# Reading the experts' bounds between pieces of the first tiles, in a two-block transformer kernel with a routed feed-forward layer

## The reference

```python
x = x + tanh(g_xattn[0]) * L0_xattn(layernorm(x), ctx)
x = x + tanh(g_ffn[0])   * L0_ffn(layernorm(x))
x = x + tanh(g_xattn[1]) * L1_xattn(layernorm(x), ctx, ctx)
x = x + tanh(g_ffn[1])   * L1_ffn(layernorm(x))       # Fourier weights

# L0_ffn, H = 256, F = 1024, E = 8, two experts a row
probs = softmax(x @ gate_w.T);  topw, sel = top_k(probs, 2);  topw /= sum(topw)
gu = einsum('th,efh->etf', x, gate_up_w);  gate, up = gu[..., :F], gu[..., F:]
expert_out = einsum('etf,ehf->eth', up * gelu(gate), down_w)
out = sum over the two experts of weight * expert_out
```

## Time and profile before

| | |
|---|---|
| median of 3 runs | 1301.15 us (1299.22 to 1301.48) |
| profiled execution, its own time | 1300.25 us |
| its span, first to last instruction | 1298.7 us |
| mean granted TensorE clock | 0.947 |
| TensorE busy | 1189.8 us, 92% |
| VectorE busy | 892.5 us, 69% |
| ScalarE busy | 569.6 us, 44% |
| first tile's load issued | 382.83 us |
| first matmul of the expert stage | 397.63 us |
| last half-tile load | 939.7 us |

### The profile page before, as it was taken

One profiled execution on the slowest core, in us unless ns is written; L12 is line 12 of the kernel. 1 busy time (PEld: TensorE's weight loads), 2 busy tenths in 40 slices (PEclk: granted clock), 3 DMA queues, 4 the chain that ended last, 5 costly groups with the idle time before them and its releaser, 6 DMA issues.

```text
span 1298.7 us, 34926 instructions
## 1 busy us (share of the span) xinstructions
PE 1189.8 (92%) x11816; PEld 992.6 (76%) x11816; DVE 892.5 (69%) x2696; ACT 569.6 (44%) x1184; POOL 263.2 (20%) x394
## 2 busy tenths in 40 slices
PE   4898989898867999999999999999997999999996
PEld 3677777776646888888888888888885777777774
DVE  4687677777645667675766767686565787787872
ACT  4565555555513242242424233242223665666652
POOL 5023242333331000000000000000004344444310
PEclk9899788888878999999999999999999999999998
DMA  9443333333433213021121313101012232222210
GB/s 293 183 162 107 117 116 124 128 101 110 150 133 138 91 37 127 33 95 61 71 94 38 122 34 126 34 25 46 26 47 81 66 93 87 81 82 85 82 34 21
DMA packets 82745, 119.58 MB, mean 92 GB/s; under 512 B 27326, under 2 KB 52558, under 8 KB 80589
## 3 DMA queue, kind: packets, MB, share of 16 engines
q1 hardware_dynamic: 64172, 60.32, 14.8%
q0 software_dynamic: 12848, 49.05, 11.3%
q10 hardware_dynamic: 5616, 8.78, 1.8%
HBM read 63.81 MB, written 47.58 MB: 86 GB/s over the span
## 4 chain that ended last, share of the span: by engine, by line
PE 80%; DVE 7%; issue 6%; SPq 2%; ACT 2%; DMA 1%; another core or an unknown queue 0%; POOL 0%; DVEq 0%; POOLq 0%; ACTq 0%
PE bank L1773 28%; PE bank L1786 14%; PE bank L1600 7%; PE bank L1534 6%; PE bank L1456 5%; PE bank L1587 3%; PE bank L1517 3%; PE bank L1519 3%; PE bank L1476 3%; PE bank L1540 2%; PE bank L1611 1%; DVE bm L1094 1%; PE bank L1598 1%; PE bank L1560 1%; PE bank L1502 1%
## 5 line engine op out<-in xcount | busy, mean ns | idle before, releaser
L1773 PE MATMUL bank<-tiles,we 128*128 128x256 f16 (+1 forms) x3744 | 392.6, 258 | 11.1 <-issue 10.2
L1773 PEld LDWEIGHTS bank<-tiles,we 128*128 128x128 f16 x3744 | 324.7, 98 | 51.1 <-issue 18.6
L947 ACT ACTIVATE tiles<-bank 128x256 f32<-128x256 f32 (+1 forms) x312 | 109.3, 353 | 330.9 <-PE bank L1773 312.2
L1786 PE MATMUL bank<-we,tiles 128*128 128x256 f16 x1608 | 223.5, 273 | 5.5 <-DVE tiles L1386 4.4
L1382 DVE SCALAR_TENSOR_TENSOR tiles<-bank,tiles 128x256 f32<-128x256 f32 (+1 forms) x312 | 120.2, 385 | 143.6 <-ACT tiles L947 138.6
L1786 PEld LDWEIGHTS bank<-we,tiles 128*128 128x128 f16 x1608 | 148.7, 98 | 40.8 <-DVE tiles L1386 17.0
L1534 PE MATMUL bank<-qT,kbd 128*128 128x256 f16 x960 | 161.6, 288 | 1.9 <-issue 1.2
L1094 DVE TENSOR_REDUCE bm<-bank 128x4 bf16<-128x308 f32 x256 | 118.2, 475 | 62.9 <-PE bank L1519 48.8
L471 DVE TENSOR_TENSOR pr<-pr 128x512 f16<-128x512 f32 x160 | 108.4, 682 | 30.9 <-ACT pr L809 25.0
L1388 DVE TENSOR_TENSOR tiles<-tiles 128x256 f16<-128x256 f32 (+1 forms) x312 | 121.1, 388 | 11.2 <-DVE tiles L1386 0.7
L1534 PEld LDWEIGHTS bank<-qT,kbd 128*128 128x128 f16 x960 | 97.4, 104 | 21.5 <-issue 1.8
(11 more groups left out here) (196 smaller groups left out, 1678.2 us busy)
## 6 DMA issues: line engine op xcount, KB each, us to landing
expert_out<-zeros SPq DMA_DIRECT2D x16, 896.0 KB
wes<-in_guT POOLq DMA_DIRECT2D x9, 1024.0 KB, 5.1
tiles<-expert_in SPq DMA_DIRECT2D x29, 256.0 KB, 2.6
pr<-in_guT POOLq DMA_DIRECT2D x7, 1024.0 KB
yg<-in_dnT POOLq DMA_DIRECT2D x7, 1024.0 KB
expert_out<-tiles ACTq DMA_DIRECT2D x28, 256.0 KB, 2.3
expert_in<-zeros POOLq DMA_DIRECT2D x8, 640.0 KB, 13.0
xin<-in_x SPq DMA_DIRECT2D x16, 256.0 KB
```

What stands on the lines that cost most here:

```text
L947: act.activation(ge[:, fc % 2, 0:n * P], bank[1 + fc % 3][:, 0:n * P], ACT.Gelu, scale=INV).then_inc(s.gelu, 1)
L1773: last = pe.matmul(bank[1 + fc % 3][:, half * S:half * S + w * P], gate_up[:, par, c, i, col:col + P], xT[:, j, c, 0:w * P], start=n == 0, ...
L1786: last = pe.matmul(bank[4 + t][:, 0:D], act16[:, fc % 4, i, t * P:(t + 1) * P], we[:, par, 2, j, fc * D:(fc + 1) * D], start=fc == 0 and n ...
```

## The change

TensorE, ScalarE and VectorE no longer read their values in one go. Each gets a function `next_bound()` that reads the next value that it has not read yet, and calls it between pieces of expert 0's first two tiles. TensorE calls it after each `up` from the third on and after each `down` (14 in tile 0, the remaining two in tile 1). VectorE calls it once at the end of each piece of tiles 0 and 1. ScalarE calls it once after each piece in tile 0 and twice in tile 1. Expert 0's bound, zero, becomes a constant on ScalarE and VectorE. SyncE's three values for expert 0 are read before `pad_first` and the wait for the scatters instead of after it.

```diff
-            def tile_rows(e):
+            def tile_bounds(e):
                 t0 = sp.value_load(tbl[0:1, bass.ds(e, 1)], min_val=0, max_val=TILES)
                 t1 = sp.value_load(tbl[0:1, bass.ds(e + 1, 1)], min_val=1, max_val=TILES)
                 tw = sp.value_load(tbl[0:1, bass.ds(e + (2 * E + 1), 1)], min_val=1, max_val=TILES)
+                return t0, t1, tw
+
+            def tile_rows(e, bounds):
+                t0, t1, tw = bounds
...
             sp.wait_ge(s.tiles_counted, 1)
+            first = tile_bounds(0)
             pad_first(sp)
             for k in range(2):
                 sp.wait_ge(s_scat[k], 64 * (NB // 2))
             sp.wait_ge(s.first_padded, 16)
-            tile_rows(0)
+            tile_rows(0, first)
             sp.wait_ge(s.padding_zeroed, 16 * (E - 1))
             with sp.Fori(1, E) as e:
-                tile_rows(e)
+                tile_rows(e, tile_bounds(e))
...
                     if part == 0 and par is not None and fc < 6:
                         next_high(e, par, fc)
+                    if e == 0 and part < 2:
+                        for _ in range(part + 1):
+                            next_bound()
                 x_hi(g + 1)
...
-            bound = [act.value_load(tbl[0:1, e:e + 1], min_val=4 if e else 0, max_val=TILES)
-                     for e in range(E + 1)]
-            end = [act.value_load(tbl[0:1, 2 * E + 1 + e:2 * E + 2 + e], min_val=3, max_val=TILES - 1)
-                   for e in range(E)]
-            offset = [act.value_load(tbl[0:1, 3 * E + 1 + e:3 * E + 2 + e], min_val=0,
-                                     max_val=OUT_ROWS - SHORT * P) for e in range(E)]
+            bound, end, offset = [0], [], []
+
+            def next_bound():
+                if len(offset) < E:
+                    e = 3 * E + 1 + len(offset)
+                    offset.append(act.value_load(tbl[0:1, e:e + 1], min_val=0, max_val=OUT_ROWS - SHORT * P))
+                elif len(bound) <= E:
+                    e = len(bound)
+                    bound.append(act.value_load(tbl[0:1, e:e + 1], min_val=4, max_val=TILES))
+                elif len(end) < E:
+                    e = 2 * E + 1 + len(end)
+                    end.append(act.value_load(tbl[0:1, e:e + 1], min_val=3, max_val=TILES - 1))
...
                             next_low(e, par, k)
                         done += LOW_PIECES[part][fc]
+                    if e == 0 and part < 2:
+                        next_bound()
                 x_low(g + 1)
...
             dve.wait_ge(s.tiles_counted, 1)
-            bound = [dve.value_load(tbl[0:1, e:e + 1], min_val=4 if e else 0, max_val=TILES)
-                     for e in range(E + 1)]
-            end = [dve.value_load(tbl[0:1, 2 * E + 1 + e:2 * E + 2 + e], min_val=3, max_val=TILES - 1)
-                   for e in range(E)]
+            bound, end = [0], []
...
-            bound = [0] + [pe.value_load(tbl[0:1, e:e + 1], min_val=1, max_val=TILES)
-                           for e in range(1, E + 1)]
-            end = [pe.value_load(tbl[0:1, 2 * E + 1 + e:2 * E + 2 + e], min_val=1, max_val=TILES)
-                   for e in range(E)]
+            bound, end = [0], []
...
                     up(par, g, fc, w)
                     if fc == 2:
                         t_x(g + 1)
+                    next_bound()
                     down(par, g, fc - 2, w)
+                    next_bound()
                 down(par, g, FC - 2, w)
+                next_bound()
                 down(par, g, FC - 1, w)
+                next_bound()
```

More of the change, by code:

```diff
@@ L940, in next_high, with expert_tile @@
                                scale=SCALE).then_inc(s.next_high, 1)
-            def expert_tile(e, g, par, part, first, t0, tw, n=QT):
+            def expert_tile(e, g, par, part, t0, n=QT):
                 for fc in range(FC):
@@ L958, in expert_tile @@
                 if n == QT:
-                    row = out_row(first + (g * S - t0 * S), S)
+                    row = out_row(offset[e] + (g * S - t0 * S), S)
                     act.dma_start(rows(ys_d, row), ysb).then_inc(s.expert_rows_stored, 16)
                 else:
-                    row = out_row(first + (g * P + tw * P - t0 * S), P)
+                    row = out_row(offset[e] + (g * P + end[e] * P - t0 * S), P)
                     act.dma_start(ys_d[bass.ds(row, P), :], ysb[:, 0]).then_inc(s.expert_rows_stored, 16)
-            bound = [act.value_load(tbl[0:1, e:e + 1], min_val=4 if e else 0, max_val=TILES)
-                     for e in range(E + 1)]
@@ L967, in _ @@
-            end = [act.value_load(tbl[0:1, 2 * E + 1 + e:2 * E + 2 + e], min_val=3, max_val=TILES - 1)
-                   for e in range(E)]
-            offset = [act.value_load(tbl[0:1, 3 * E + 1 + e:3 * E + 2 + e], min_val=0,
-                                     max_val=OUT_ROWS - SHORT * P) for e in range(E)]
-            def expert(e, par):
[L973 to L979, removed]
+            bound, end, offset = [0], [], []
@@ L981, in _ @@
+            def expert(e, par):
+                t0 = bound[e]
+                expert_tile(e, t0, par, 0, t0)
+                expert_tile(e, t0 + 1, par, 1, t0)
+                with act.Fori(t0 + 2, end[e]) as g:
+                    expert_tile(e, g, par, 2, t0)
+                with act.Fori(end[e], bound[e + 1]) as g:
+                    expert_tile(e, g, par, 2, t0, 1)
             x_hi(0)
@@ L1393, in expert_tile, with next_bound @@
                         done += LOW_PIECES[part][fc]
+                    if e == 0 and part < 2:
+                        next_bound()
                 x_low(g + 1)
             def expert(e, par):
-                t0, t1, tw = bound[e], bound[e + 1], end[e]
+                t0 = bound[e]
                 expert_tile(e, t0, par, 0)
                 expert_tile(e, t0 + 1, par, 1)
-                with dve.Fori(t0 + 2, tw) as g:
+                with dve.Fori(t0 + 2, end[e]) as g:
                     expert_tile(e, g, par, 2)
-                with dve.Fori(tw, t1) as g:
+                with dve.Fori(end[e], bound[e + 1]) as g:
                     expert_tile(e, g, par, 2, 1)
             dve.wait_ge(s.tiles_counted, 1)
-            bound = [dve.value_load(tbl[0:1, e:e + 1], min_val=4 if e else 0, max_val=TILES)
-                     for e in range(E + 1)]
-            end = [dve.value_load(tbl[0:1, 2 * E + 1 + e:2 * E + 2 + e], min_val=3, max_val=TILES - 1)
-                   for e in range(E)]
+            bound, end = [0], []
+            def next_bound():
+                if len(bound) <= E:
+                    e = len(bound)
+                    bound.append(dve.value_load(tbl[0:1, e:e + 1], min_val=4, max_val=TILES))
+                elif len(end) < E:
+                    e = 2 * E + 1 + len(end)
+                    end.append(dve.value_load(tbl[0:1, e:e + 1], min_val=3, max_val=TILES - 1))
             x_low(0)
@@ L1789, in down, with next_bound @@
                 last.then_inc(s.down, 1)
-            bound = [0] + [pe.value_load(tbl[0:1, e:e + 1], min_val=1, max_val=TILES)
-                           for e in range(1, E + 1)]
-            end = [pe.value_load(tbl[0:1, 2 * E + 1 + e:2 * E + 2 + e], min_val=1, max_val=TILES)
-                   for e in range(E)]
+            bound, end = [0], []
+            def next_bound():
+                if len(bound) <= E:
+                    e = len(bound)
+                    bound.append(pe.value_load(tbl[0:1, e:e + 1], min_val=1, max_val=TILES))
+                elif len(end) < E:
+                    e = 2 * E + 1 + len(end)
+                    end.append(pe.value_load(tbl[0:1, e:e + 1], min_val=1, max_val=TILES))
             def tile(e, g, w):
```

## The result

The changed kernel takes 1288.58 us (median of 6 runs, 1285.64 to 1291.53) against 1300.54 for the kernel before (median of 6 on the same chip, 1299.22 to 1304.1): ratio 0.9908, 95% interval 0.9891 to 0.9924. That is 12.0 us, between 9.9 and 14.2. The profiled execution is the fastest of the six, 1285.64 us with a span of 1284.1; mean granted clock 0.953.

What follows compares the result with a forecast made beforehand. The prediction took the engines' `tbl` reads ahead of expert 0's first tile as the bound; 11.3 (start) + 1.45 (clock) - 0.85 (added) = 11.9 us gained, giving 1289.3 us, range 1286.8 to 1293.8 with rivals.

Steps and rivals of the forecast that it cites:

- What bounds it: Ahead of expert 0's first tile: TensorE's `tbl` loads hold `t_x(0)` and ScalarE's hold `x_hi(0)`; the wait is not for data.
- SyncE: Before the first tile's load: reads move ahead of the padding, which becomes the last wait; worth 0.5 us, not 1.7.
- The new start: First matmul of expert 0's first tile at about 386.3 instead of 397.63: gain 11.3 us.
- The clock: First 36 matmuls at full clock take 4.09 us instead of 5.79; less 0.25 lost, net gain 1.45 us.
- Rival 1: At the first tile the clock falls all the same, costing 1.7 to 3.4 us: 1291.0 to 1292.7; chance 0.2.
- the one at 984.8: Stretch of the profile before with TensorE busy 1.74 us and 1.66 idle, where the clock kept 1.00.
- What it adds: Reads between pieces of tiles 0 and 1 cost 0.35 + 0.4 + 0.1 = 0.85 us; bounds nothing and 10.5.
- Rival 2: In tile 0 each of eight loads behind a `down` costs 0.66, 5.3 us for 0.75 counted: 1293.8; chance 0.12.
- rival 3: Slower: each load among engine instructions waits until its engine has drained, 5.9 us above now: 1307; chance 0.03.
- What it triggers: Tile 1's load runs beside GpSimd's 1 MB fetch, landing at 388.5 or 391.4; taken as nothing, 0.9 kept for the range.
- The range: Forecast's own range for the kernel's time: 1287.3 (nothing added and 1 us between runs) to 1290.9 (late tile load and 0.7).

Runs made afterwards that it cites:

- SyncE's part alone: Kernel before with only SyncE's three reads of expert 0 moved ahead of the padding, the other engines reading in one go; ratio 1.0004.
- TensorE's with SyncE's: Changed kernel, but ScalarE's 24 and VectorE's 16 reads stand in one go ahead of the first tile; ratio 0.9998.
- the three engines' together: Changed kernel with SyncE's reads put back where they were in the kernel before; ratio 0.9924.
- The run with the padding first: Changed kernel with the padding's DMA issued ahead of SyncE's three reads, which still precede the wait for the scatters; ratio 0.9903.
- The sixteen reads in a row: Changed kernel with TensorE's 16 reads all behind up(4) of tile 0 instead of one behind each piece; ratio 0.9989.

## Why the prediction was right

The time on record, 1289.3, lies 0.7 above the measured median; the forecast gain was 11.9 and the measured one 12.0, with an interval of over 2 us on either side. The traces give 10.6, and one term of the sum was wrong by more than the number is off: by the prediction's own price for a falling clock, 1.7 at least, the time would have been 1291.0 or more. So the closeness to 0.7 us is luck; that the start is what the reads hold, and that reads between pieces cost next to nothing, is not. By the steps:

- *What bounds it.* Right. SyncE's part alone and TensorE's with SyncE's give nothing (ratios 1.0004 and 0.9998), and the three engines' together give nearly all.
- *SyncE.* Right: the load at 5.25 for a forecast of 5.2 (382.3 less 377.1), and the padding as the new last wait. The run with the padding first shows what that order costs: 1.3 us at the first matmul, and 3.0 at tile 1 (25.32 against 28.29), since the clock held there.
- *The new start.* 11.3 forecast, 11.05 and 10.9 in the two pairs of traces. The transposes came 0.2 late: the load landed after 2.65 and not 2.56, and 0.14 went by behind it.
- *The clock.* This step failed: 1.45 forecast, -0.3 and -0.1 in the two pairs (the block from the first matmul to the second transposes took 5.63 and 5.62 before, 5.92 and 5.71 after). Rival 1, given 0.2, is what happened in both profiles of the changed kernel and in that without SyncE's part. The price I gave it, 1.7 at least, is about what the comparison with the held clock shows: 5.92 and 5.71 against 4.25, so 1.7 and 1.5. The reason given for the chance, that the new stretch would be like the one at 984.8, did not hold.
- *What it adds.* 0.85 forecast, 0.35 measured: tile 0 from its second transposes 12.46 to 12.89, tile 1 from 16.54 to 16.46. The end of tile 0 cost the 0.4 that I counted. The 0.35 after `down(0)` did not come, with the clock fallen or, in the runs with the padding first, held: I had shifted the activation with the matmuls that it followed, but the ACT_TABLE_LOAD no longer waits for them. It runs at 385.13, straight behind `x_hi`, and not after the first piece of `up`, which brings the first Gelu forward by up to its 1.28 us. It isn't where the reads stand that does this: with ScalarE's reads in one go ahead of `x_hi` it also runs straight behind it (397.18 + 0.60, 397.79). What these kernels share, and the kernel before and SyncE's part alone lack, is expert 0's bound as a constant; I had costed that edit at nothing. The traces show where the wait stands: before the change ScalarE's queue waits for the first piece of `up` in an operation of its own (L946, at 400.4), and the table load comes behind it; after it the wait goes with the ACTIVATE behind the table load. That the constant is what moves the wait is argued from these four, not tried by itself. `x_low(2)` cost nothing.
- *Rivals 2 and 3.* Rival 2 had 5.3 us for the reads behind `down`, and 0.35 is there. The sixteen reads in a row refute rival 3 directly, and the lead of 2.1 us that they show is what hides the single ones. (Its 0.25 us for filling the array again was not measured; the earlier trace rows have 0.27 for one matmul. Nothing else hangs on it.) From the Trainium skill, TensorE: Matmul & The Clock Gate, on engine queue depths, the prediction had estimated 3.5 us; the lead here is 2.1, and the measurement decides.
- *What it triggers.* The fetch and tile 1's load ran together; the load landed after 3.0 us (median before 2.6), 387.7, with 3.4 us to spare (second transposes at 391.13).
- *The range.* Its lower end adds up to 1287.45 and not 1287.3 (1289.3 less 0.85 and 1); nothing hangs on it.

So the sum of the traces is 11.05 - 0.3 - 0.35 = 10.4 at tile 2, 1.5 less than forecast: 1.75 by the clock and 0.25 by the start, with 0.5 given back by cheaper reads. Why the medians gained more than the traces show at the end of the stage (12.0 against 10.6, and 14.7 against 10.6 on the other chip) was not settled; both are inside the intervals.

## What to carry to other kernels

A register read cost its queue 0.53 to 0.73 us here, and the engine nothing so long as the queue was that far ahead: put such reads between pieces of work, one at a time, and not behind a piece that ends in a wait or ahead of a stage's first. When several queues do the same in front of one stage, the gain is there only once all of them are freed. And when work is moved ahead of a wait, look at what it is moved ahead of: here a DMA of 256 KB that then became the wait, for 1.3 us. Whether the clock held was worth 1.5 to 1.7 us, more than all the reads between pieces cost (0.35).

## What the runs showed of the hardware that I had not expected

- Whether the clock fell went with the pause ahead of the first transposes. It held after 0.74 (twice), 1.02, 1.11 and 1.89 us, and was at 0.50 soon after 2.01, 2.12, 2.42, 2.91 and 3.05 us. These ten traces show the two going together, but they give no limit: the work on either side of the pause may count as well.
- With extra matmuls in TensorE's program the padding landed later: after 4.5, 3.5 and 3.9 us for 2.0 without them. In each of these three traces 135 of the padding's 144 packets start in their usual time, and the last nine, 16 KB, only when one packet of the instruction queue (16 KB) has ended: it starts at 4.8, 3.6 and 3.7 after the table's write and lasts 0.9, 1.4 and 1.6 us, and the nine start at 5.7, 5.0 and 5.3. In the changed kernel that packet comes at 11.5, with no padding to hold up. The extra matmuls themselves start only at 5.6 to 5.7, behind the packet, so it isn't their running that delays the padding. Their records number 38, 20 and 20; what calls the packet forth so early is open.
- The same kernel before took 1300.5 and 1300.6 us in two of the comparisons and 1240.8 and 1240.5 on two other chips. From 120 to 240 us, in layer 0's attention, the granted clock is 0.83 in the trace before, and 1.00 in that of SyncE's part alone from one of the faster chips; from the first instruction to the table's write it is 377 us against 322. Every ratio above is taken on one chip.
